# The first norm's rows normalised by ScalarE instead of VectorE in a fused attention and expert block

## What is computed

```python
def _layernorm(x, axis=-1, eps=1e-05):
    m = jnp.mean(x, axis=axis, keepdims=True)
    v = jnp.var(x, axis=axis, keepdims=True)
    return (x - m) / jnp.sqrt(v + eps)
...
    h = _layernorm(x, axis=-1) * (1 + ca) + sa
    x = x + ga * _L0_attn_ref(h, ...)
    h = _layernorm(x, axis=-1) * (1 + cb) + sb
    x = x + gb * _L0_ffn_ref(h, ...)
```

## Time and profile before

| | us |
|---|---|
| median of 3 runs | 2449.8 |
| lowest and highest | 2448.88, 2453.46 |
| the profiled execution | 2457.11 |
| its span, first to last instruction | 2455.3 |
| TensorE busy in the span | 2372.7 (97%) |
| VectorE busy | 1569.8 (64%) |
| ScalarE busy | 1032.8 (42%) |
| GpSimd busy | 1149.7 (47%) |

### The profile page before, as it was taken

How to read it: one execution, slowest core, us unless ns; L and a number is a source line. 1 busy time by engine, 2 the same in 40 slices (tenths; PEclk the granted TensorE clock), 3 DMA queues, 4 the chain that set the end, 5 groups by cost and what they waited for, 6 DMA issues and landing times.

```text
span 2455.3 us, 40998 instructions
## 1 busy us (share of the span) xinstructions
PE 2372.7 (97%) x14388; PEld 2087.3 (85%) x14388; DVE 1569.8 (64%) x3198; ACT 1032.8 (42%) x1912; POOL 1149.7 (47%) x997
## 2 busy tenths in 40 slices
PE   6999999999998999999988999999999999999997
PEld 5788888888887888888877888888888888888886
DVE  5667767777786778788858545555555545555553
ACT  3455545445453545445443333333333333333332
POOL 0233333333332333333344666666666666666664
PEclk8999999999998999999999999999999999999999
DMA  2111111111111111111224444444344444444433
GB/s 83 44 61 60 51 51 64 48 60 51 55 63 39 52 60 60 52 53 52 69 78 90 83 86 86 86 87 82 62 86 85 86 85 88 84 61 87 84 63 43
DMA packets 78538, 167.03 MB, mean 68 GB/s; under 512 B 11776, under 2 KB 46752, under 8 KB 78400
## 3 DMA queue, kind: packets, MB, share of 16 engines
q0 software_dynamic: 49152, 67.14, 17.0%
q1 hardware_dynamic: 29248, 97.85, 11.8%
HBM read 97.71 MB, written 67.24 MB: 67 GB/s over the span
## 4 chain that ended last, share of the span: by engine, by line
PE 83%; DVE 7%; issue 5%; POOL 2%; DMA 1%; ACT 1%; SPq 0%; DVEq 0%; POOLq 0%
PE ps L354 26%; PE ps L356 26%; PE ps L355 26%; PE ps L506 2%; DVE stage L861 2%; PE ps L392 1%; DVE bn_stats L763 1%; DMA x_rows<-h_rows,step_token 1%; PE ps L425 1%; DVE x_t L758 1%; POOL rstd L1151 1%; PE ps L447 1%; DVE hidden L758 1%; POOL out L1216 1%; POOL x_rows L1169 0%
## 5 line engine op out<-in xcount | busy, mean ns | idle before, releaser
L354 PE MATMUL ps<-x_t,weights 128*128 128x512 f32 x1536 | 615.8, 401 | 8.4 <-issue 5.9
L355 PE MATMUL ps<-x_t,weights 128*128 128x512 f32 x1536 | 601.4, 392 | 0.0
L356 PE MATMUL ps<-x_t,weights 128*128 128x512 f32 x1536 | 600.6, 391 | 0.0
L1216 POOL DMA_INDIRECT out<-x_rows,step_token x256 | 417.8, 1632 | 322.1 <-DVE x_rows L1095 263.3
L354 PE MATMUL ps<-weights,hidden 128*128 128x256 f32 x1536 | 435.5, 284 | 6.3 <-POOL hidden L1155 2.7
L356 PE MATMUL ps<-weights,hidden 128*128 128x256 f32 x1536 | 435.5, 284 | 0.0
L355 PE MATMUL ps<-weights,hidden 128*128 128x256 f32 x1536 | 435.5, 284 | 0.0
L1118 DVE TENSOR_TENSOR hidden_f<-gelu,ps 128x512 f32<-128x512 f32 x256 | 175.7, 686 | 380.7 <-ACT gelu L738 332.8
L738 ACT ACTIVATE gelu<-ps 128x512 f32<-128x512 f32 x256 | 152.8, 597 | 541.8 <-PE ps L356 516.2
L1155 POOL TENSOR_TENSOR hidden<-hidden_f,hidden 128x512 fp32r<-128x512 f32 x128 | 165.4, 1292 | 407.0 <-ACT hidden L652 407.0
L354 PEld LDWEIGHTS ps<-x_t,weights 128*128 128x128 f32 x1536 | 290.2, 189 | 68.4 <-issue 8.7
(11 more groups left out here) (174 smaller groups left out, 4450.0 us busy)
## 6 DMA issues: line engine op xcount, KB each, us to landing
pairs<-mod_rows SPq DMA_DIRECT2D x36, 512.0 KB, 4.3
x_rows<-in_x SPq DMA_DIRECT2D x32, 512.0 KB, 3.5
h_rows<-stage SPq DMA_DIRECT2D x32, 512.0 KB, 2.6
out<-y_rows SPq DMA_DIRECT2D x32, 512.0 KB, 2.9
stage<-in_wg SPq DMA_DIRECT2D x16, 512.0 KB, 3.7
stage<-in_wd SPq DMA_DIRECT2D x16, 512.0 KB, 4.5
stage<-in_wu SPq DMA_DIRECT2D x16, 512.0 KB
x_rows<-h_rows,step_token POOLq DMA_INDIRECT x256
```

Source lines behind the costliest of these rows:

```text
L354: pe.matmul(o, lhs(HI), rhs(HI), start=start, stop=False)
L355: pe.matmul(o, lhs(HI), rhs(LO), start=False, stop=False)
L356: return pe.matmul(o, lhs(LO), rhs(HI), start=False, stop=stop)
L1216: pool.indirect_dma_start(out=out_rows, out_offset=bass.IndirectOffsetOnAxis(ap=ICUR[g][:, t:t + 1], axis=0), in_=X1[:, g % 2, t * D:(t + ...
```

## The change

VectorE's `ln1_apply` is gone. ScalarE gets a function of that name: four ACTIVATE of 128x256 with the function Identity, scale `rstd` and bias `-mean * rstd`, both read per partition, from `X` to `XN`. It stands behind `hidden(i - 1, 0)`, so behind the first gelu and the copy of its product, and ahead of `squares`. For the bias there is a new tile, `NMR`, and a semaphore, `nmr1`. GpSimd computes it: the mean times -1 ahead of `rstd`, and the product with `rstd` behind it (`centre`).

```diff
+            def ln1_apply(n, p):
+                act.wait_ge(nmr1, n + 1)
+                wait(act, xt_done, n)
+                for t in range(T):
+                    last = act.activation(XN[:, t, :], X[:, p, t * D:(t + 1) * D], ACT.Identity,
+                                          bias=NMR[:, t:t + 1], scale=RS[0][:, t:t + 1])
+                last.then_inc(xn_ready, 1)
...
                     hidden(i - 1, 0)
+                if valid(i + 1):
+                    ln1_apply(i + 1, 1 - p)
                 if valid(i):
                     squares(i, (0, 1))
...
-            def ln1_apply(n, p):
-                dve.wait_ge(rs1, n + 1)
-                wait(dve, xt_done, n)
-                for t in range(T):
-                    last = dve.tensor_scalar(XN[:, t, :], X[:, p, t * D:(t + 1) * D], MV[0][:, t, 0:1],
-                                             RS[0][:, t:t + 1], ALU.subtract, ALU.mult)
-                last.then_inc(xn_ready, 1)
...
                     weights_lo(i, (2, 3))
-                if valid(i + 1):
-                    ln1_apply(i + 1, 1 - p)
...
+            def centre(n):
+                pool.wait_ge(rs1, n + 1)
+                pool.tensor_tensor(NMR[:, :], NMR[:, :], RS[0][:, :], ALU.mult).then_inc(nmr1, 1)
...
                 if valid(i + 1):
+                    wait_apart(pool, mv1, i + 2)
+                    pool.tensor_scalar(NMR[:, :], MV[0][:, :, 0], -1.0, None, ALU.mult)
                     rstd(0, mv1, ve1, rs1, i + 1)
+                    centre(i + 1)
```

More of the change, by code:

```diff
@@ L118, in block_kernel @@
         RS = [sb(f"rstd{j}", [P, T]) for j in range(2)]
+        NMR = sb("neg_mean_rstd", [P, T])
         NM = sb("neg_max", [P, T])
@@ L161, in block_kernel @@
         mod_in = [sem("mod_in0"), sem("mod_in1")]
-        st1, mv1, ve1, rs1, xn_ready = map(sem, ("st1", "mv1", "ve1", "rs1", "xn_ready"))
+        st1, mv1, ve1, rs1, nmr1, xn_ready = map(sem, ("st1", "mv1", "ve1", "rs1", "nmr1", "xn_ready"))
         xt_done, h1f_ready, h1_hi, h1_lo = map(sem, ("xt_done", "h1f_ready", "h1_hi", "h1_lo"))
```

## The result

| | median us | range, runs | ratio to before, 95% interval |
|---|---|---|---|
| before | 2453.85 | 2446.94 to 2460.99, 22 | |
| changed | 2461.82 | 2456.51 to 2469.01, 22 | 1.0035, 1.0026 to 1.0044 |

The change makes the kernel 0.35% slower, and the interval lies clear of no change; 0.3% was forecast. The profiled execution has a span of 2462.1 us where that of before had 2455.3.

The account below looks back on a forecast made before the run. TensorE, busy 97% of the span, was taken to bound the kernel. Transposes' added waits, less gains at start-up and iterations 18 and 26, summed to +7 us: 2449.8 + 7 = 2456.8 us, 0.3% slower, range 2448 to 2463.

Parts of the forecast that it names:

- not removed but exchanged: TensorE's stall at the transposes stays: rows come later than before, by 0.22 us with constant counts, 0.38 in loops.
- g: The end of an iteration's first gelu on ScalarE, from which the prediction counts times; TensorE is free at g + 2.61.
- Rival A: Register waits cost nothing at VectorE's gelu product (0.03 in loops): sum +3.6, 2453.4 us; chance with its kin 0.28.
- four in 1.94 us: ScalarE's four norm ACTIVATE at 0.56 us each, less three overlaps of 0.10; bounds 1.23 and 2.80.
- rival C: ScalarE's norm ACTIVATE is dearer from SBUF, up to 0.776 us: +26, 2483; 0.03 more each: 2460.4; upper end's chance 0.02.
- Rival B: Per-partition operands cost nothing from SBUF (0.383 us per ACTIVATE): sum -13, 2437; chance 0.09, shared with a start-up gaining more.
- At the transposes: TensorE's added wait for ScalarE's norm: 20 loop iterations x 0.38 = +7.6 us, six with constants x 0.22 = +1.3.
- The ends of the best-token passes: At the end of iterations 18 and 26, ScalarE's squares come about 0.75 us sooner: -1.5 for both.
- Start-up: VectorE's four norm instructions (1.37 us) leave the chain ahead of TensorE's first K: -1.3 us.
- 0.35 us at worst: Least time to spare for GpSimd's bias, hidden by the gelu's chain; without that cover each 0.1 us costs 3 us.
- Rival D: GpSimd's addition gets ahead of VectorE's gelu product and blocks it: +60 us or more, 2510; chance 0.01.

Follow-up runs that it names:

- Experiment 2: The kernel before, with GpSimd's addition of the output rows made to wait until VectorE's norm of the same iteration is done: 2431.54 us, ratio 0.9912 to before.
- experiment 3: The changed kernel with constant scale 1 and bias 0 in ScalarE's four norm instructions, rows left unnormalised: 2437.62 us, ratio 0.9946 to the kernel before.
- experiment 4: The kernel before, with ScalarE's norm in the start-up alone: ratio 0.9997 to before; together with the wait of Experiment 2: 0.9905.
- Experiment 5: The changed kernel with one more power of 128x4 on GpSimd between rstd and bias: 1.0034 to before; its last kernel, with two more: 1.0112.

## Why the prediction was right, point by point

**Where TensorE stood still and why.** It held at the transposes. Experiment 2 shows that the addition stretched the norm's first instruction. Elsewhere TensorE didn't run quite back to back, as the prediction had it: see "Not foreseen" below. That a kernel that lost 29 stretched instructions still became slower is the prediction's "not removed but exchanged".

**When the norm can start.** Forecast g + 1.26 with constants and g + 1.42 in loops; measured g + 1.28 and g + 1.44. Rival A, that a register's wait costs nothing at this place, is out: the two kinds of iteration differ by the 0.16 us read from the earlier trace rows.

**How long it takes.** Forecast four in 1.94 us, measured 2.07. This is the one mis-sized term. The step was 776 - 215 = 561 ns, with the price of columns taken from a gelu and a square; the measured instruction takes 587. The prediction had allowed for up to 0.03 us more on each (with rival C); no run changed the source of the instruction alone, so whether SBUF is the reason stays open. With the formula from the Trainium skill, "ScalarE: Activation LUTs", section "What ACT_TABLE_LOAD costs", which the prediction quotes, the trace agrees: it gives an estimate of 585 ns, and 587 was measured; with constants it gives 399, and experiment 3 measured 402. By that estimate the forecast would have been 2460.3 in place of 2456.8. Rival B needed 0.383; experiment 3's 0.402 shows that this price is about right only without the operands. The 0.49 us at which rival B has the loops break even is where the whole sum does; the loops alone break even at 0.47 (g + 1.42, plus four of 0.47 less 3 x 0.10, is g + 3.00, where VectorE's norm had ended at g + 2.98).

**The sum.** Between the transposes of one iteration and the next, the two traces differ as follows; measured in the starts of TensorE's instructions.
- At the transposes, in the 20 loop iterations 0.51 us more each (0.74 to 1.25 between starts), where 0.38 was forecast: +10.3 for +7.6. With constants 0.35 for 0.22: +2.1 for +1.3. Iterations 18 and 26 +0.14, iteration 30 +0.04, iteration 1 +0.8. But for iteration 30 it is 0.13 to 0.17 more than forecast in each place: the four instructions' 0.13 and 0.02 at the start. At iterations 18 and 26, forecast within 0.1 of nothing, that same excess is the 0.14.
- The ends of the best-token passes: forecast -1.5, measured -1.0 in each of the two iterations, -2.0.
- Start-up: forecast -1.3. The first K came 1.4 us sooner, at 23.38 for 24.79 in the earlier trace rows, and the transposes of sequence 1 2.7 us sooner, 49.56 for 52.25. The 2.7 us enter the difference of the spans, but experiment 4 shows that one trace can't tell the change's part of them from the clock's.
- Not foreseen: -2.3. In 18 iterations, from the first with best-token rounds on, TensorE had a small wait of about 0.13 ahead of the third quarter of the shared expert, for VectorE's product of the second. It went when VectorE's queue got shorter. Before, and then in the changed kernel:

```profile
663.30 0.68 DVE L875 TENSOR_TENSOR hidden_f<-gelu,ps 128x512 f32<-128x512 f32 x1
...
664.13 0.47 PE L354 MATMUL ps<-x_t,weights 128*128 128x512 f32 x1
664.43 0.39 PE L355 MATMUL ps<-x_t,weights 128*128 128x512 f32 x1
```

```profile
666.93 0.68 DVE L878 TENSOR_TENSOR hidden_f<-gelu,ps 128x512 f32<-128x512 f32 x1
...
668.86 0.40 PE L355 MATMUL ps<-x_t,weights 128*128 128x512 f32 x1
669.10 0.40 PE L356 MATMUL ps<-x_t,weights 128*128 128x512 f32 x1
```

Before, the product ended 0.15 ahead of the matmul that needs it, and that matmul came 0.08 late; now it ends 1.25 ahead. The two matmuls start 0.30 apart before and 0.24 apart after. In experiment 2, where VectorE's norm takes 1.38 in place of 3.45, what is left of the wait is at most 0.06 in 17 of the 18. It is too small for a row of its own among the waits, and so was overlooked.

These add up to +6.6 of the 6.8 between the spans. What is left is small and cancels: -1.1 at the end of the last best-token pass, about +1.1 in phase B, which the change doesn't touch. So that the total met the forecast is in part luck: two errors of opposite sign, the dearer instruction (+4) and the unseen wait with the larger gain at the passes and the start (-4), left the forecast of +7 standing. The ratio over 22 runs, +0.35% or 8.6 us, lies 1.6 above it. The median of 2461.82 lies 5.0 above the forecast 2456.8, and 4 of that is the baseline: 2453.85 over 22 runs of the kernel before, where the prediction had 2449.8 from three.

**What was hidden.** GpSimd's product cost nothing, and had far more cover than "0.35 us at worst": it took 0.20 and left 1.2 us (1.36 in loops). Experiment 5 used up a microsecond of it for nothing, and beyond it each 0.1 us did cost 3 us in all. Rival D is out: the gelu's product started at 658.77 under an addition that had begun at 658.61, and took its 0.69. The gate scores' product was stretched in each of the 29 iterations with the addition, mostly to 1.15 in the loops and 1.4 with constants; the median of 1.16 is a little less than the 1.3 to 2 forecast. K's input was split 0.7 us sooner after the gelu in the second loop (g + 6.47 for g + 7.14) and under 0.1 sooner in the first, not 1 us, because ScalarE's `h1_modulate` now comes last there. Nobody waited for it.

## What to carry to other kernels

An operation that leaves a busy engine helps only if its new place in the other queue is ready sooner: work out the chain of what stands ahead of it, waits included, against the moment at which the consumer comes free. Here one place in ScalarE's queue was worth 1.4%. And when an instruction is much longer in one surrounding than its own median, look at what starts with it on a neighbour engine first: a wait of one semaphore on the neighbour gave 0.9% where moving the work away to the place chosen lost 0.35%.

## What the runs showed of the hardware

- A wait with the count in a register, in an instruction of its own, put the next instruction 0.16 to 0.19 us later than one with a constant: VectorE's product at g + 0.03 or g + 0.18, the transposes 0.05 or 0.24 behind the norm's end. Where the instruction carried its wait itself, there was no difference: ScalarE's norm, with the register instruction ahead of it and the wait on the ACTIVATE, started 0.03 behind the bias in both kinds of iteration in the last kernel of experiment 5.
- GpSimd's multiplication of 128x4 takes 0.20 us, its power 1.01 to 1.04.
- The granted clock in the first 60 us was 0.83 in one execution and 0.96 in another, with sequence 1's transposes 6.5 us apart under the same start-up. A profile of one execution can't price a start-up edit of 1 or 2 us.
- In the start-up's second application the same ScalarE instruction took up to 647 ns in place of 587. No run tells why.
